# Projecting the keys and values of the last attention during the routing stage before it

## The chip, the cores and the metric

The kernel runs on one core of one Trainium2 chip. The metric is the device time of one execution in microseconds (us); three runs of the kernel before gave 3404.11 to 3409.8, with a median of 3405.26.

## The reference, cut to what matters

A stream `x` of 16 batches, 112 tokens and 256 features passes four layers, each an attention to a fixed context and a feed-forward part. The kernel computes them as eight stages, one after the other. The change is in stage 5 (a feed-forward part with routed experts) and stage 6 (the attention of the fourth layer, here the narrow attention: 16 heads of 16 features, against 64 features in the wide attention of stage 4).

```
x = x + L2_ffn(layernorm(x))                       # stage 5: top 2 of 8 experts for each token
x = x + L3_xattn(layernorm(x), ctx, ctx, mask)     # stage 6

# L3_xattn, per batch; ctx is 375 x 256 and is an input, D_K = 16
q = query @ Wq.T + bq
k = ctx @ Wk.T + bk
v = ctx @ Wv.T + bv
scores = q k^T / sqrt(D_K), -1e9 where mask == 0
out = softmax(scores) v, heads joined, @ Wo.T + bo
```

Keys and values depend on the context and the weights alone, not on `x`.

## The kernel before, in words

The program is written engine by engine: in each stage every engine (TensorE `pe`, VectorE `dve`, ScalarE `act`, GpSimd `pool`, SyncE `sp` for the DMAs) has its own list of instructions, and semaphores order them against each other. `after(eng, sem, n)` waits only where `n` is over zero. Between stages stands a barrier of all engines (`core.clear()`). There is no planner: the order on each engine is the order in the code. `each_batch` runs a body for batches 0 and 1, a hardware loop for 2 to 13 and the body twice more.

**Routing** (`route`, L1705) comes before the experts and has its own barrier behind it. SyncE loads the router's weights and fills the DRAM buffer of the experts' rows with zeros in four DMAs (L1768). For each batch TensorE transposes the normalized tokens (L1938) and computes 8 logits a token (L1931); ScalarE evicts the transposes (L1795), VectorE takes the logits. After the last batch VectorE alone finds the best two experts (L1846 to L1856), TensorE multiplies the choices by a triangular matrix and by ones (L1946, L1947), VectorE turns the sums into positions up to the put list (L1919), and GpSimd scatters the tokens by 32 indirect DMAs (L1779). ScalarE has one exponential between (L1799). Then come the expert matmuls (`run_experts`; its first DMA is L2000) and `combine`.

**Narrow attention** (`softmax_attention` with `wide` false, L781). The opening loads the weights (L924), folds the value bias into the output bias (L1281, L1070), and projects batch 0. Then each batch goes through its 16 heads in pairs. For a pair TensorE multiplies scores into two PSUM banks (L1232). VectorE adds the mask and takes the minimum (L1100), after which TensorE may write the next pair's scores into the same banks. ScalarE takes the exponential (L1038), TensorE transposes the probabilities of the pair before (L1242), VectorE copies the transposes to SBUF (L1111), and after every second pair TensorE multiplies four heads of transposed probabilities by the values (L1258). Those four products write to four different groups of 32 output partitions.

Between these steps stand jobs, at fixed heads in `slots` (L808). They go through two further PSUM banks in turn:

```python
slots = [[K[0]], [], [K[1]], [], [Q[0]], [], [Z], [], [V[0]], [], [Y], [], [V[1]], [], [X], []]
```

K, Q and V project keys, queries and values of the batch after (L1183, L1189, L1194), X transposes the tokens two batches ahead (L1200), Z spreads the reciprocal sums of the batch before and Y multiplies its output by `Wo`. ScalarE evicts K (L999), Q (L1008), V (L1014) and X (L1024), each in its own place between two exponentials. GpSimd spreads the queries into a block-diagonal form (L961), which the scores need. The values lie 32 columns wide for each head, 16 of them zero (memset L953). The last batch has no successor, so no K, Q, V or X job stands in it. SyncE loads context and mask for two batches in turn (L928, L931).

## Time and profile before

| What | Value |
|---|---|
| Median of three runs | 3405.26 us |
| The profiled execution: its time, its span | 3406.88 us, 3404.9 us |
| Mean granted TensorE clock | 0.878 |
| Second routing stage | 2180.0 to 2282.1 |
| Experts and combine of the same layer | 2282.1 to 2702.6 |
| Narrow attention | 2702.6 to 3138.8 |

The stages' borders are where SyncE issues the first DMA of a stage. Times in the rows are us from the span's start. PE is TensorE's matmul, PEld its weight load, DVE VectorE, ACT ScalarE, POOL GpSimd, SPq SyncE's queue. A float32 matmul has two records, so "x8" is four matmuls. In a timeline row stand the start, the time until the last of the merged instructions ends, engine and line, the tiles (out<-in) and, in brackets, the idle time before it with what ended it. [...]

### The profile page before, as it was taken

How to read it: one execution, taken by the hardware profiler on the slowest of the kernel's cores; microseconds unless marked ns; L12 is line 12 of the kernel's file. 1: busy time of each engine (PE TensorE's matmuls, PEld its weight loads, DVE VectorE, ACT ScalarE, POOL GpSimd, SP SyncE). 2: the span in 40 equal slices, each digit the busy share in tenths (PEclk: the TensorE clock that was granted, in tenths of full speed). 3: DMA queues.
4: the chain of work that ended last, by engine and by line, in shares of the span. 5: the costliest groups of instructions: out<-in, count | busy, mean ns of one | idle time of the engine just before them, and what ended most of it. 6: DMA issues, size and time to landing. Idle time of an engine off the chain costs nothing. (4 is left out here: it accounts for less than half of the span.)

```text
span 3404.9 us, 48975 instructions
## 1 busy us (share of the span) xinstructions
PE 2571.2 (76%) x15414; PEld 1780.1 (52%) x15414; DVE 1525.1 (45%) x5311; ACT 1089.5 (32%) x2415; POOL 621.5 (18%) x739
## 2 busy tenths in 40 slices
PE   3775249999478699699999999619996199997232
PEld 3664237777334355356665666418885066665121
DVE  5887612222334443333333333411111666766877
ACT  3443001111079501244444444202221055554121
POOL 0000030000322000144444444330002211111000
PEclk8888569999789889899999999759998599999555
DMA  2111033221121100100000000135553100000000
GB/s 70 45 45 53 29 136 102 78 74 51 50 71 63 51 0 0 65 10 10 5 9 9 9 9 0 66 103 178 184 173 110 53 28 20 24 21 26 0 0 22
DMA packets 62522, 174.60 MB, mean 51 GB/s; under 512 B 13531, under 2 KB 32760, under 8 KB 52952
## 3 DMA queue, kind: packets, MB, share of 16 engines
q1 hardware_dynamic: 52344, 148.58, 13.2%
q0 software_dynamic: 10080, 24.79, 2.3%
q8 instruction: 52, 0.85, 0.1%
q14 instruction: 46, 0.38, 0.0%
HBM read 143.98 MB, written 29.36 MB: 51 GB/s over the span
## 5 line engine op out<-in xcount | busy, mean ns | idle before, releaser
L2131 PE MATMUL L_ffne_up<-L_ffne_xT,L_ffne_wu 128*128 128x280 f32 (+1 forms) x1696 | 406.6, 399 | 23.8 <-DVE L_ffne_xT L2057 15.5
L2131 PEld LDWEIGHTS L_ffne_up<-L_ffne_xT,L_ffne_wu 128*128 128x128 f32 x1696 | 325.6, 193 | 95.2 <-ACT L_ffne_hT L2044 17.5
L1094 DVE TENSOR_REDUCE L_xattn_least<-L_xattn_s 112x1 f32<-112x375 f32 x256 | 128.4, 543 | 440.3 <-PE L_xattn_s L1232 440.3
L948 POOL TENSOR_SCALAR L_xattn_p<-L_xattn_p,L_xattn_rec 112x375 f32<-112x375 f32 x256 | 313.2, 1231 | 0.0
L2117 PE MATMUL L_ffne_dn<-L_ffne_wd,L_ffne_hT 128*128 128x256 f32 (+1 forms) x1312 | 288.1, 379 | 1.6 <-issue 1.6
L1242 PEld LDWEIGHTS L_xattn_pt<-ident,L_xattn_p 112*125 112x125 f32 x1536 | 191.4, 189 | 152.5 <-issue 108.7
L2117 PEld LDWEIGHTS L_ffne_dn<-L_ffne_wd,L_ffne_hT 128*128 128x128 f32 (+1 forms) x1312 | 241.1, 184 | 44.3 <-issue 2.4
L1242 PE MATMUL L_xattn_pt<-ident,L_xattn_p 112*125 112x112 f32 x1536 | 243.3, 291 | 7.6 <-POOL L_xattn_p L948 7.4
L1111 DVE COPY L_xattn_pt<-L_xattn_pt 125x336 f32<-125x336 f32 x512 | 232.7, 495 | 6.4 <-PE L_xattn_pt L1242 6.2
L1183 PE MATMUL L_xattn_job<-L_xattn_ctxT,L_xattn_wk 128*128 128x375 f32 x640 | 221.7, 486 | 1.8 <-ACT L_xattn_xt L1021 0.9
L1194 PE MATMUL L_xattn_job<-L_xattn_wv,L_xattn_ctxT 128*125 128x512 f32 (+1 forms) x576 | 220.1, 523 | 2.1 <-ACT L_xattn_v L1014 0.7
L1038 ACT ACTIVATE L_xattn_p<-L_xattn_s,L_xattn_least 112x375 f32<-112x375 f32 x256 | 145.7, 570 | 188.4 <-DVE L_xattn_least L1094 188.4
L1038 ACT ACTIVATE L_xattn_p<-L_xattn_ssb,L_xattn_least 112x375 f32<-112x375 f32 x256 | 154.4, 603 | 141.3 <-DVE L_xattn_least L1100 134.4
L2020 POOL DMA_DIRECT2D L_ffn_ybuf<-L_ffne_y x82 | 43.8, 535 | 720.0 <-DVE L_ffne_y L2069 405.6
L1100 DVE CUSTOM_DVE_ANT_0 L_xattn_ssb<-L_xattn_s,L_xattn_hide 112x375 f32<-112x375 f32 x256 | 130.8, 544 | 90.4 <-issue 90.4
L2042 ACT ACTIVATE L_ffne_sg<-L_ffne_up 128x280 f32<-128x280 f32 x128 | 51.6, 403 | 349.2 <-PE L_ffne_up L2131 349.2
L2044 ACT ACTIVATE L_ffne_hT<-L_ffne_up,L_ffne_b 128x256 f32<-128x256 f32 x168 | 79.2, 473 | 233.6 <-PE L_ffne_up L2131 231.2
L1258 PE MATMUL L_xattn_o<-L_xattn_pt,L_xattn_v 125*64 125x112 f32 (+1 forms) x3072 | 152.9, 267 | 0.6 <-DVE L_xattn_pt L1111 0.6
L946 POOL TENSOR_TENSOR pool_tick<-ident 1x1 f32<-1x1 f32 x128 | 23.4, 183 | 700.3 <-DVE L_xattn_rec L1106 700.3
L1258 PEld LDWEIGHTS L_xattn_o<-L_xattn_pt,L_xattn_v 125*64 125x64 f32 (+1 forms) x3072 | 110.3, 124 | 76.1 <-issue 56.9
L2087 DVE TENSOR_TENSOR L_ffne_hT<-L_ffne_sg,L_ffne_up 128x280 f32<-128x280 f32 x128 | 57.1, 446 | 205.2 <-ACT L_ffne_sg L2042 205.2
L1183 PEld LDWEIGHTS L_xattn_job<-L_xattn_ctxT,L_xattn_wk 128*128 128x128 f32 x640 | 115.9, 193 | 62.9 <-issue 2.5
(326 smaller groups left out, 4122.7 us busy)
## 6 DMA issues: line engine op xcount, KB each, us to landing
L_ffne_wd<-in_L_ffn_down SPq DMA_DIRECT2D x29, 1024.0 KB, 4.8
L_ffne_wu<-in_L_ffn_up SPq DMA_DIRECT2D x21, 1024.0 KB, 5.5
L_ffne_wu<-in_L_ffn_up SPq DMA_DIRECT2D x8, 2048.0 KB, 7.7
L_xattn_ctxT<-in_ctxT SPq DMA_DIRECT2D x32, 375.0 KB, 3.1
fa_ctxT<-in_ctxT SPq DMA_DIRECT2D x16, 375.0 KB, 6.3
fa_rows<-in_ctx_rows SPq DMA_DIRECT2D x16, 375.0 KB
ta_kT<-in_ctxT SPq DMA_DIRECT2D x16, 375.0 KB
ta_ctxr<-in_ctx_rows SPq DMA_DIRECT2D x16, 375.0 KB
```

Source lines behind the costliest of these rows:

```text
L948: p = pool.tensor_scalar(p_sb[:, head % RP, :], p_sb[:, head % RP, :], rec[:, h, head:head + 1], None, ALU.mult)
L1038: act.activation(p_sb[:, head % RP, :], src, ACT.Exp, bias=least[:, h, head:head + 1], scale=-1.0, accum_out=sums[:, h, head:head + 1]).th ...
L1094: dve.tensor_reduce(low, s, AX.X, ALU.min).then_inc(low_done, 1)
L1100: dve.tensor_tensor_reduce(out=ssb[:, head % 4, :], in0=s, in1=hide[:, h, :], scale=1.0, scalar=3e38, op0=ALU.add, op1=ALU.min, accum_out= ...
L1111: dve.tensor_copy(pt_sb[:, head % RP, :, :], pt_ps[head % 2][0:KP, 0, 0:KT * S].rearrange("p (k s) -> p k s", k=KT)).then_inc(pt_done, 1)
L1183: m = pe.matmul(ps[:, 0, 0:SK], wk[:, c, i * 128:(i + 1) * 128], ctxT[:, h, c, :], start=(c == 0), stop=(c == DC - 1))
L1194: m = pe.matmul(ps[0:KP, 0, n * VW:(n + 1) * VW], ctxT[:, h, c, kt * KP:(kt + 1) * KP], wv[:, c, w * VW:(w + 1) * VW], start=(c == 0), sto ...
L1242: m = pe.transpose(pt_ps[head % 2][0:KP, 0, kt * S:(kt + 1) * S], p_sb[:, head % RP, kt * KP:(kt + 1) * KP], ident[0:S, 0:S])
L1258: m = pe.matmul(o_ps[n * VC:(n + 1) * VC, chunk // 4, chunk % 4 * S:(chunk % 4 + 1) * S], v_sb[:, h, kt, head_at(head + n), :], pt_sb[:, ( ...
L2044: act.activation(hT[:, h, f, q * RH:(q + 1) * RH], src, ACT.Gelu, bias=b1[:, h, f:f + 1]).then_inc(h_done, 1)
L2117: m = pe.matmul(dn_ps[i][0:TR, 0, 0:D], hT[:, h, f, t * TR:(t + 1) * TR], wd[:, h, f, :], start=(f == 0), stop=(f == FC - 1))
L2131: m = pe.matmul(up_ps[s % RING][k][:, 0, 0:RH], wu[:, h, c, k * FF + f * 128:k * FF + (f + 1) * 128], xT[:, h, c, q * RH:(q + 1) * RH], st ...
```

## The change

A class `KeysValues` holds keys and values of all 16 batches in SBUF (97,152 bytes on a partition). The second routing stage opens it: SyncE loads the key and value weights and the context of two batches ahead of the zero fills, and the other 14 behind them. TensorE projects batches 0 and 1 between the last logits and the cumulative matmuls, and the other 14 after these; ScalarE evicts batches 0 and 1 ahead of the exponential of the gaps. In the narrow attention the jobs K and V go, and with them the context loads, the `wk` and `wv` loads and GpSimd's memset of the values. The products read 16 columns of values for each head; VectorE clears the output bank once in their place. TensorE's body is written out for all 16 batches instead of looping, since it addresses keys and values by batch. The job Q waits for the X job's eviction, which the K job did before. The bodies on the other engines keep their loops.

```diff
@@ -805,7 +806,7 @@
         slots = [[K[0]], [K[1]], [K[2]], [K[3]], [K[4]], [K[5], K[6]], [K[7]], [], [Q[0]], [Q[1]], [Y],
                  [V[0]], [V[1], V[2]], [V[3]], [V[4], V[5]], [X]]
     else:
-        slots = [[K[0]], [], [K[1]], [], [Q[0]], [], [Z], [], [V[0]], [], [Y], [], [V[1]], [], [X], []]
+        slots = [[], [], [], [], [Q[0]], [], [Z], [], [], [], [Y], [], [], [], [X], []]
     order = [j for jobs in slots for j in jobs]
     LT = 4 if wide else 2
     LP = 6
...
@@ -912,29 +914,29 @@
         with nc.Block() as block:
             @block.sync
             def _(sp):
-                loads = [(wq[:, :, :], ins[pre + "_Wq"]), (wk[:, :, :], ins[pre + "_Wk"]),
-                         (wv[:, :, :], ins[pre + "_Wv"]), (wo[:, :, :], ins[pre + "_Wo"]),
+                loads = [(wq[:, :, :], ins[pre + "_Wq"]), (wo[:, :, :], ins[pre + "_Wo"]),
                          (bias_y[:, :], ins[pre + "_bo"].partition_broadcast(S))]
                 if wide:
+                    loads += [(wk[:, :, :], ins[pre + "_Wk"]), (wv[:, :, :], ins[pre + "_Wv"])]
                     loads += [(gb[:, 0, :], ins[pre + "_gamma"]), (gb[:, 1, :], ins[pre + "_beta"]),
                               (gate[:, 0:1], ins["L2_xattn_gate"].partition_broadcast(128))]
                 else:
-                    loads += [(bq[:, :], ins[pre + "_bq"]), (bk[:, :], ins[pre + "_bk"]), (bv[:, :], ins[pre + "_bv"])]
+                    loads += [(bq[:, :], ins[pre + "_bq"]), (bv[:, :], ins[pre + "_bv"])]
                 for to, src in loads:
                     sp.dma_start(to, src).then_inc(w_in, 16)
                 def load(b, h):
-                    after(sp, out["v"], (b - 1) * NV)
-                    sp.dma_start(ctxT[:, h, :, :], ins["ctxT"][b]).then_inc(ctx_in[h], 16)
-                    if not wide:
+                    if wide:
+                        after(sp, out["v"], (b - 1) * NV)
+                        sp.dma_start(ctxT[:, h, :, :], ins["ctxT"][b]).then_inc(ctx_in[h], 16)
+                    else:
                         after(sp, mask_done, b - 1)
                         sp.dma_start(msk[:, h, :], ins["mask"][b]).then_inc(ctx_in[h], 16)
                 each_batch(sp, load)
-            CTX = 16 if wide else 32
-            NLOADS = 8
+            NLOADS = 8 if wide else 5
             def wait_ctx(eng, b, h):
-                eng.wait_ge(ctx_in[h], (b - h) * (CTX // 2) + CTX)
+                eng.wait_ge(ctx_in[h], (b - h) * 8 + 16)
             @block.gpsimd
             def _(pool):
...
@@ -1015,7 +1011,10 @@
                                                ps[0:KP, 0, n * VW:(n + 1) * VW].rearrange("p (h d) -> p h d", h=hs),
                                                ACT.Copy)
                     elif kind == "x":
-                        after(act, out["v"], (b - 1) * NV)
+                        if wide:
+                            after(act, out["v"], (b - 1) * NV)
+                        else:
+                            after(act, out["q"], b - 1)
                         for c in range(DC):
                             if wide:
                                 r = act.activation(xt[:, h, c, :], ps[:, 0, c * S:(c + 1) * S], ACT.Identity,
...
@@ -1066,6 +1065,7 @@
                     ch.link(dve.tensor_scalar(bias_y[:, :], bias_y[:, :], gate[0:S, 1:2], None, ALU.mult))
                 else:
                     dve.wait_ge(w_in, NLOADS * 16)
+                    dve.memset(o_ps[:, 0, :], 0.0).then_inc(pad_done, 1)
                     dve.wait_ge(bias_out, 1)
                     dve.tensor_tensor(bias_y[:, :], job_ps[0][0:S, 0, 0:D], bias_y[:, :], ALU.add).then_inc(bias_done, 1)
                     dve.wait_ge(bias_done, 1)
...
@@ -1183,6 +1183,8 @@
                             m = pe.matmul(ps[:, 0, 0:SK], wk[:, c, i * 128:(i + 1) * 128], ctxT[:, h, c, :],
                                           start=(c == 0), stop=(c == DC - 1))
                     elif kind == "q":
+                        if not wide:
+                            pe.wait_ge(done["x"], b + 1)
                         for n in range(QB):
                             for c in range(DC):
                                 at = (i * QB + n) * 128
...
@@ -1228,7 +1230,7 @@
                         if wide:
                             q, k = qt[r, h, n // 2, :], kt_sb[r, h, n // 2, :]
                         else:
-                            q, k = qbd[r, h, n // HG, n % HG // 2, :], kt_sb[r, h, n // HG, :]
+                            q, k = qbd[r, h, n // HG, n % HG // 2, :], keys.kt[r, b, n // HG, :]
                         m = pe.matmul(s_ps[n % 2][0:S, 0, 0:SK], q, k, start=True, stop=True)
                     m.then_inc(s_out, 2)
...
@@ -1255,8 +1257,10 @@
                     chunk = head // SIDE
                     for kt in range(KT):
                         for n in range(SIDE):
-                            m = pe.matmul(o_ps[n * VC:(n + 1) * VC, chunk // 4, chunk % 4 * S:(chunk % 4 + 1) * S],
-                                          v_sb[:, h, kt, head_at(head + n), :], pt_sb[:, (head + n) % RP, kt, :],
+                            hd = head_at(head + n)
+                            v = v_sb[:, h, kt, hd, :] if wide else keys.v[:, b, kt, hd * dh:(hd + 1) * dh]
+                            m = pe.matmul(o_ps[n * VC:n * VC + dh, chunk // 4, chunk % 4 * S:(chunk % 4 + 1) * S],
+                                          v, pt_sb[:, (head + n) % RP, kt, :],
                                           start=(kt == 0), stop=(kt == KT - 1))
                     m.then_inc(pv_out, SIDE)
@@ -1282,9 +1286,14 @@
                                       start=(c == 0), stop=(c == OC - 1))
                     m.then_inc(bias_out, 1)
                     pe.wait_ge(bias_done, 1)
+                    pe.wait_ge(pad_done, 1)
                 pe.wait_ge(xn_done, 1)
                 projections(job)
-                each_batch(pe, body)
+                if wide:
+                    each_batch(pe, body)
+                else:
+                    for b in range(NB):
+                        body(b, b % 2)
                 for head in range(LT):
                     turn_p(NB - 1, 1, H + head - LT)
                 for head in range(10 if wide else 12, H, SIDE):
...
@@ -1675,6 +1684,67 @@
                         m.then_inc(dn_out, 1)
+class KeysValues:
+
+
+    def __init__(self, core, ctx, pre):
+        self.pre = pre
+        self.kt = core.sb(ctx, pre + "_kt", [128, NB, DC, SK])
+        self.v = core.sb(ctx, pre + "_v", [KP, NB, KT, D])
+
+    def open(self, core, ctx):
+
+        pre = self.pre + "kv_"
+        self.wk, self.wv = core.sb(ctx, pre + "wk", [128, DC, D]), core.sb(ctx, pre + "wv", [128, DC, D])
+        self.bk = core.sb(ctx, pre + "bk", [128, DC])
+        self.ctxT = core.sb(ctx, pre + "ctxT", [128, 2, DC, SK])
+        self.ps = [core.banks(ctx, f"{pre}ps{i}", 1) for i in range(2)]
+        self.w_in, self.ctx_in = core.sem(ctx, pre + "w_in"), [core.sem(ctx, f"{pre}ctx_in{i}") for i in range(2)]
+        self.out, self.done = core.sem(ctx, pre + "out"), core.sem(ctx, pre + "done")
+        self.parts = [("k", 0), ("k", 1), ("v", (0, 1)), ("v", (2,))]
+
+    def load_weights(self, sp, ins):
+        for to, src in ((self.wk, "_Wk"), (self.wv, "_Wv")):
+            sp.dma_start(to[:, :, :], ins[self.pre + src]).then_inc(self.w_in, 16)
+        sp.dma_start(self.bk[:, :], ins[self.pre + "_bk"]).then_inc(self.w_in, 16)
+
+    def load(self, sp, ins, b):
+        n = len(self.parts)
+        after(sp, self.out, (b - 1) * n)
+        sp.dma_start(self.ctxT[:, b % 2, :, :], ins["ctxT"][b]).then_inc(self.ctx_in[b % 2], 16)
+
+    def project(self, pe, b):
+
+        h, n = b % 2, len(self.parts)
+        pe.wait_ge(self.ctx_in[h], (b - h) * 8 + 16)
+        for i, (kind, part) in enumerate(self.parts):
+            after(pe, self.done, b * n + i - 1)
+            ps = self.ps[i % 2]
+            if kind == "k":
+                for c in range(DC):
+                    m = pe.matmul(ps[:, 0, 0:SK], self.wk[:, c, part * 128:(part + 1) * 128], self.ctxT[:, h, c, :],
+                                  start=(c == 0), stop=(c == DC - 1))
+            else:
+                for at, kt in enumerate(part):
+                    for c in range(DC):
+                        m = pe.matmul(ps[0:KP, 0, at * D:(at + 1) * D], self.ctxT[:, h, c, kt * KP:(kt + 1) * KP],
+                                      self.wv[:, c, :], start=(c == 0), stop=(c == DC - 1))
+            m.then_inc(self.out, 1)
+
+    def take(self, act, b):
+
+        n = len(self.parts)
+        for i, (kind, part) in enumerate(self.parts):
+            act.wait_ge(self.out, b * n + i + 1)
+            ps = self.ps[i % 2]
+            if kind == "k":
+                r = act.activation(self.kt[:, b, part, :], ps[:, 0, 0:SK], ACT.Identity, bias=self.bk[:, part:part + 1])
+            else:
+                r = act.activation(self.v[:, b, part[0]:part[0] + len(part), :].rearrange("p k d -> p (k d)"),
+                                   ps[0:KP, 0, 0:len(part) * D], ACT.Copy)
+            r.then_inc(self.done, 1)
+
+
 class Routing:
...
@@ -1762,11 +1835,18 @@
                 else:
                     sp.dma_start(more[:, :], ins[pre + "_router_b"].partition_broadcast(S)).then_inc(w_in, 16)
+                if keys:
+                    keys.load_weights(sp, ins)
+                    keys.load(sp, ins, 0)
+                    keys.load(sp, ins, 1)
                 sp.wait_ge(setup, 2)
                 flat = r.xbuf.rearrange("(p n) d -> p (n d)", p=128)
                 for q in range(4):
                     sp.dma_start(flat[:, q * fill_w:(q + 1) * fill_w], zeros[:, :]).then_inc(filled, 16)
                 sp.wait_ge(filled, 64)
+                if keys:
+                    for b in range(2, NB):
+                        keys.load(sp, ins, b)
             @block.gpsimd
             def _(pool):
@@ -1795,8 +1875,15 @@
                     act.activation(xt[:, h, :, :], xt_ps[h][:, 0, 0:DC * S].rearrange("p (c s) -> p c s", c=DC),
                                    ACT.Copy).then_inc(x_done, 1)
                 each_batch(act, body)
+                if keys:
+                    act.wait_ge(keys.w_in, 48)
+                    for b in range(FIRST):
+                        keys.take(act, b)
                 act.wait_ge(gap_done, 1)
                 act.activation(gap[:, :], gap[:, :], ACT.Exp).then_inc(gap_exp, 1)
+                if keys:
+                    for b in range(FIRST, NB):
+                        keys.take(act, b)
             @block.vector
             def _(dve):
@@ -1941,10 +2028,17 @@
                         logits(b - 1, 1 - h)
                 each_batch(pe, body)
                 logits(NB - 1, 1)
+                if keys:
+                    pe.wait_ge(keys.w_in, 48)
+                    for b in range(FIRST):
+                        keys.project(pe, b)
                 pe.wait_ge(picked_done, 1)
                 flat = picked[:, :, :].rearrange("p b e -> p (b e)")
                 pe.matmul(cum_ps[0:S, 0, 0:NE], before[:, :], flat, start=True, stop=True)
                 pe.matmul(cum_ps[0:S, 1, 0:NE], ones[:, :], flat, start=True, stop=True).then_inc(cum_out, 1)
+                if keys:
+                    for b in range(FIRST, NB):
+                        keys.project(pe, b)
 def run_experts(core, pre, r, gated):
...
@@ -2243,6 +2337,14 @@
         for layer in LAYERS:
             PARTS[layer](core)
             core.clear()
+        with ExitStack() as kept:
+            keys = KeysValues(core, kept, "L3_xattn")
+            routed_experts(core, "L2_ffn", False, keys)
+            core.clear()
+            softmax_attention(core, "L3_xattn", keys)
+            core.clear()
+        ternary_ffn(core)
+        core.clear()
         store_output(core, out)
...
```

## Rows read from the trace of the kernel before

**Rows 1.** Windows: us; busy us (xcount) of PE, PEld, DVE, ACT, POOL; PEclk; DMA.
```profile
2219.30:2282.10 62.80, 1.20 (x5) 0.88 (x4) 13.31 (x99) 0.55 (x2) 30.23 (x32) 0.50 0.20 59
2725.06:3108.23 383.17, 381.09 (x3284) 248.20 (x3283) 264.18 (x1084) 206.54 (x630) 63.69 (x59) 1.00 0.07 21
3108.23:3126.46 18.23, 16.62 (x162) 10.79 (x158) 15.19 (x65) 9.12 (x28) 1.04 (x1) 1.00 0.01 1
```

**Rows 2.** Timeline of the second routing stage's end: start, busy time, engine, line.
```profile
2217.74 1.57 PE L1931 MATMUL L_ffnr_lg<-L_ffnr_wr,L_ffnr_xt 128*112 128x8 f32 x8
...
2234.65 0.18 DVE L1919 CAST L_ffn_put<-L_ffnr_slot 112x32 uint32<-112x32 f32 x1
...
2274.47 0.94 POOL L1779 DMA_INDIRECT L_ffn_xbuf<-L_ffn_xf,L_ffn_put  x1 [0.30 <-issue]
2282.10 0.40 SPq L2000 DMA_DIRECT2D L_ffne_rows<-L_ffn_xbuf  x1
```

**Rows 3.** Timeline of TensorE over one looped batch of the narrow attention.
```profile
2850.14 0.89 PE L1232 MATMUL L_xattn_s<-L_xattn_kt,L_xattn_qbd 64*112 64x375 f32 x4
...
2851.70 1.44 PE L1183 MATMUL L_xattn_job<-L_xattn_ctxT,L_xattn_wk 128*128 128x375 f32 x4
2853.07 0.89 PE L1232 MATMUL L_xattn_s<-L_xattn_kt,L_xattn_qbd 64*112 64x375 f32 x4
...
2856.89 0.89 PE L1232 MATMUL L_xattn_s<-L_xattn_kt,L_xattn_qbd 64*112 64x375 f32 x4
...
2862.89 0.89 PE L1232 MATMUL L_xattn_s<-L_xattn_kt,L_xattn_qbd 64*112 64x375 f32 x4
...
2864.45 1.90 PE L1194 MATMUL L_xattn_job<-L_xattn_wv,L_xattn_ctxT 128*125 128x256 f32 x8
2866.28 0.89 PE L1232 MATMUL L_xattn_s<-L_xattn_kt,L_xattn_qbd 64*112 64x375 f32 x4
...
2870.64 0.89 PE L1232 MATMUL L_xattn_s<-L_xattn_kt,L_xattn_qbd 64*112 64x375 f32 x4
...
2872.20 1.04 PE L1194 MATMUL L_xattn_job<-L_xattn_wv,L_xattn_ctxT 128*125 128x256 f32 x4
2873.41 0.89 PE L1232 MATMUL L_xattn_s<-L_xattn_kt,L_xattn_qbd 64*112 64x375 f32 x4 [0.17 <-DVE L_xattn_least L1100]
...
2875.25 0.78 PE L1258 MATMUL L_xattn_o<-L_xattn_pt,L_xattn_v 125*32 125x112 f32 x24
2876.00 0.89 PE L1232 MATMUL L_xattn_s<-L_xattn_kt,L_xattn_qbd 64*112 64x375 f32 x4
```

**Rows 4.** The same view over the stage's last batch.
```profile
3108.23 0.89 PE L1232 MATMUL L_xattn_s<-L_xattn_kt,L_xattn_qbd 64*112 64x375 f32 x4
...
3110.26 0.89 PE L1232 MATMUL L_xattn_s<-L_xattn_kt,L_xattn_qbd 64*112 64x375 f32 x4 [0.30 <-DVE L_xattn_least L1100]
...
3112.62 0.89 PE L1232 MATMUL L_xattn_s<-L_xattn_kt,L_xattn_qbd 64*112 64x375 f32 x4
...
3119.93 0.89 PE L1232 MATMUL L_xattn_s<-L_xattn_kt,L_xattn_qbd 64*112 64x375 f32 x4 [0.30 <-DVE L_xattn_least L1100]
...
3124.03 0.89 PE L1232 MATMUL L_xattn_s<-L_xattn_kt,L_xattn_qbd 64*112 64x375 f32 x4
```

**Rows 5.** Timeline of the narrow attention's opening.
```profile
2710.84 3.75 PE L1281 MATMUL L_xattn_job<-L_xattn_wo,L_xattn_bv 128*112 128x256 f32 x8 [99.58 <-DMA L_xattn_bv<-in_L_xattn_bv]
...
2721.17 1.82 POOL L961 TENSOR_TENSOR L_xattn_qbd<-L_xattn_qt,halfmask 128x448 f32<-128x448 f32 x2 [17.17 <-ACT L_xattn_qt L1008]
```

**Rows 6.** Groups of the narrow attention; DMA issues, the last number is us to landing.
```profile
L999 ACT ACTIVATE L_xattn_kt<-L_xattn_job,L_xattn_bk 128x375 f32<-128x375 f32 x32 | 18.3, 572 | 22.4 <-PE L_xattn_job L1183 22.4
...
L_xattn_ctxT<-in_ctxT SPq DMA_DIRECT2D x32, 375.0 KB, 3.1
fa_ctxT<-in_ctxT SPq DMA_DIRECT2D x16, 375.0 KB, 6.3
...
L_ffn_xbuf<-L_ffnr_zeros SPq DMA_DIRECT2D x4, 1344.0 KB, 10.1
```

More of the change, by code:

```diff
@@ L796, in softmax_attention @@
     VW = 512 if wide else D
-    NK, NQ = IC, IC // QB
-    v_parts = [[(kt, w)] for kt in range(KT) for w in range(inner // VW)] if wide else [[(0, 0), (1, 0)], [(2, 0)]]
+    NK, NQ = IC if wide else 0, IC // QB
+    v_parts = [[(kt, w)] for kt in range(KT) for w in range(inner // VW)] if wide else []
     NV = len(v_parts)
@@ L952, in _ @@
                     return
-                pool.memset(v_sb[:, :, :, :, dh:VC], 0.0).then_inc(setup, 1)
                 def body(b, h):
@@ L994, in job @@
                         after(act, s_out, (b - 1) * H)
-                        to, src = kt_sb[:, h, i, :], ps[:, 0, 0:SK]
-                        if wide:
-                            r = act.activation(to, src, ACT.Copy)
-                        else:
-                            r = act.activation(to, src, ACT.Identity, bias=bk[:, i:i + 1])
+                        r = act.activation(kt_sb[:, h, i, :], ps[:, 0, 0:SK], ACT.Copy)
                     elif kind == "q":
@@ L1248, in products @@
                     pe.wait_ge(pt_done, b * H + head + SIDE)
-                    if head == 0:
+                    if wide and head == 0:
                         pe.wait_ge(done["v"], made("v", b, NV - 1))
```

36 lines of the change are left out of this document (19 added, 17 removed).

## The prediction

> **What bounds the kernel now.** I read the table of windows first, one window for each stage that the change touches. In the narrow attention TensorE is busy 381.09 of 383.17 us at clock 1.00, while VectorE has 264.18 and ScalarE 206.54 [rows 1]. TensorE is the bound there, and the key and value projections are part of what it does. In the second half of the second routing stage it is the other way round: TensorE works 1.20 us in a window of 62.80, at clock 0.50 [rows 1]. What sets the end of that window is a chain: the last logits end at 2217.74 + 1.57 = 2219.3, VectorE writes the put list at 2234.65, GpSimd issues 32 scatters, the last at 2274.47, and SyncE's first DMA of the expert stage goes out at 2282.10 [rows 2]. So the change moves TensorE work from a stage that it bounds into a hole of 62.8 us. The two questions are how much the donor gives back and whether the hole is large enough.
>
> **What one batch of projections costs.** In the looped batch at 2850.14 a key part stretches the distance between two TensorE steps by 2853.07 - 2851.70 = 1.37 us; there are two. The first value part is 2866.28 - 2864.45 = 1.83, the second 1.04 by its row [rows 3]. I take 1.0 for it, since a row's busy time runs a little over the distance. Sum: 2 x 1.37 + 1.83 + 1.0 = 5.57 us a batch at clock 1.00; 16 batches are 89.1 us.
>
> **Narrow attention, what it gives back.** A batch takes 2876.00 - 2850.14 = 25.86 us now [rows 3]. Taking off 5.57 would leave 20.3, but that holds only if TensorE never waits for anything else. The last batch of the stage shows what a batch without these jobs is like, for it has no successor to project for [rows 4]. Its first pair, with no job at all, takes 3110.26 - 3108.23 = 2.03 us, and the next scores stood 0.30 us waiting for VectorE's minimum L1100: scores, two passes of VectorE, scores again are a loop of 2.03 us which no idle TensorE shortens. Pair by pair, before against the last batch:
> - heads 0, 1: 2853.07 - 2850.14 = 2.93 against 2.03; VectorE answers a little later in the loop's body, so I count 2.08: -0.85
> - heads 2, 3: 2856.89 - 2853.07 = 3.82 against 3112.62 - 3110.26 = 2.36: -1.46
> - heads 4 to 7: query and reciprocal jobs stay: 0
> - heads 8, 9: 2866.28 - 2862.89 = 3.39 against 2.03: -1.36
> - heads 10, 11: 2870.64 - 2866.28 = 4.36 against 3124.03 - 3119.93 = 4.10: -0.26, the transposes no longer stall behind a value eviction
> - heads 12, 13: the second value part sits here, but the next scores already waited 0.17 us for VectorE [rows 3], which is at the residual of the batch before. That residual stays: 0
> - heads 14, 15: 0
>
> That is 3.93 us a batch, period 21.9. Fifteen batches carry jobs for a successor: 15 x 3.93 = 59.0. The remaining 1.64 us a batch turn into waits for L1100. The bounds are 3.4 (every light pair held by VectorE for 0.2 us more than in the last batch) and 5.57 (no wait at all): 51 and 84 us.
>
> The prologue: queries of batch 0 stand behind two key parts, and GpSimd's two block-diagonal products, 1.82 us from 2721.17 [rows 5], behind them. Without key parts they start 2.6 us earlier and end at 2720.4; the first scores followed value parts and started at 2725.06, where a window of [rows 1] begins; now they follow GpSimd at once: -4.6. The weight loads shrink by two of 256 KB and the one of the key bias, three issue slots of 0.4 to 0.5 us and a third of the bytes ahead of the bias matmul at 2710.84 [rows 5]: I take -1.9, between 0 and -3. The queries' new wait for their x tile finds it written in the turn before; the memset of the output bank (one VectorE pass, estimated at under 1 us) lies beside the 3.75 us bias matmuls. TensorE now stands some 2.5 us before the first scores and may start them at the lower clock: +1, between 0 and +2. Masks alone are left on SyncE's queue; nobody waited for it. TensorE's body written out sixteen times costs nothing by [rows 3, 4]: the written-out last batch has no gap that another engine doesn't explain.
> Sum of the stage: -59.0 - 4.6 - 1.9 + 1 = -64.5.
>
> **Routing, what it takes.** SyncE issues three weight loads and two context loads ahead of the four zero fills: five slots, 2 to 2.5 us, and 1.3 MB of traffic ahead of them. A fill lands 10.1 us after its issue [rows 6], around 2193, and is needed by the scatters only after 2234.65; 40 us cover it. The context of batches 0 and 1 is in SBUF long before 2219.3. Then the matmuls: 89.1, plus the slow start. The eight 256-column records at 2710.84 took 3.75 us on an engine that came from idling [rows 5]; eight such took 1.90 at clock 1.00 [rows 3]: +1.9. The two cumulative matmuls between batches 1 and 2 are part of 1.20 us at half clock: 0.6. End of the last projection: 2219.3 + 89.1 + 1.9 + 0.6 = 2310.9, its eviction 2311.4, the barrier some 1 us (below 6.7, since 2282.10 - 2275.41 held a landing as well): 2312.4 against 2282.1, +30.3.
> Batches 0 and 1 also stand in front of the cumulative matmuls and, on ScalarE, in front of the exponential of the gaps; VectorE's position chain and then the scatters wait behind these. They take 2 x 5.57 + 1.9 = 13.0 us from 2219.3, so the put list is at most 13 us late and the scatter's end at most at 2295. That is 16 us before TensorE is through: the delay is hidden by the other 14 batches and costs nothing. ScalarE evicts a key part in 0.57 us [rows 6] against the 1.37 that TensorE needs for the next part, so two banks suffice.
> Each context load may start when TensorE takes up the batch before, and has 5.57 us. The attention stages' loads land 3.1 us after issue; those of the first stage, which share the queues with as large a second stream, 6.3 [rows 6]. With a slot of 0.4 that is 3.5 to 6.7 us. The scatters move 112 rows of 1 KB each 1.25 us, 90 GB/s. I take the near row, 3.1: hidden. At the far end it costs (6.7 - 5.57) x 14 = 16 us.
>
> **Sum.** -64.5 + 30.3 = -34.2. The profiled execution took 3406.88 (span 3404.9 and 2 around it): 3372.7. It is 1.6 above the median of 3405.26, so I predict 3371.
>
> **Rivals.**
> *TensorE's time comes back whole.* VectorE's waits shrink with TensorE's, 5.57 a batch: 25 us more, 3346. Against it: the 2.03 us pairs and their wait of 0.30 in the last batch, where nothing else was in the way. Chance 0.05.
> *The context loads bound the projections.* 6.3 us each: 3387. For it: the scatters' descriptors and these loads run at once. Against: 375 KB in 5.57 us are 69 GB/s. Chance 0.10.
> *Slower: the narrow attention falls to half clock.* TensorE, dense now, gets gaps of 0.3 to 1.2 us in three or four pairs of every batch. [...] Against it: the last batch has 16.62 busy of 18.23 us and the granted clock stands at 1.00 [rows 1]. Chance 0.04.
> [...]
> *Slower: the products lose their packing.* The output products now take 16 columns of weights in place of 32. Twelve such matmuls (24 records), at four output offsets, fit into 2876.00 - 2875.25 = 0.75 us today [rows 3]. One by one, at a 256-column record's 1.83 / 8 us scaled to 112 columns, 0.10 each, they would take 2.4: +1.65, four times a batch, 106 over the stage: 3477. It decides against the change from a group time of 0.75 + 34 / 64 = 1.3 us. No row shows 16 columns. Chance 0.03.
>
> **How the numbers follow.** The forecast has 0.75, and by its bounds (attention 51 to 64 us from the pairs, clock and barrier a few us) runs from 3360 to 3382. With the loads' case to the upper side and half of the way to the first rival on the lower one, the range is 3358 to 3388. A kernel that projects as said but gains within 0.2% (7 us, about what a measurement of this kernel can tell from no change), by several small losses: 0.03. Faster 0.75 + 0.05 + 0.10 = 0.90, same 0.03, slower 0.04 + 0.03 = 0.07.
>
> **What would show it.** Expert stage's first DMA at 2312, put list written at 2243 to 2248, TensorE's last projection at about 2311 with clock 1.00 but for its first few us. Period of a narrow batch 21.9, pairs of heads 0, 1 and 8, 9 at 2.03 to 2.2 with waits for L1100. If the period is under 21 the VectorE loop was no bound; if the projections take over 6 us a batch with TensorE waiting for a DMA, the loads are; if the clock of the narrow stage is under 0.95, or a group of twelve products takes over 1 us, one of the slower cases holds.

## The result, and the profile after

The changed kernel takes 3371.47 us, median of four runs (3369.47 to 3374.87), against 3405.22 for the kernel before on the same chip: a ratio of 0.9894, 95% interval 0.9879 to 0.9909, 33.8 us less. Forecast were 3371, range 3358 to 3388, and faster with a chance of 0.90. The profiled execution has a span of 3369.6.

The windows of the changed kernel, one a stage, show where the time went. The columns are those of [rows 1], where PEclk is the TensorE clock that was granted, as a share of its full speed; the first two windows are the second routing stage's first half and its projections, then come the expert combination, the opening of the narrow attention, its batch 0 and its batches 1 to 13 with most of 14 (a batch runs from its first scores to the next batch's).

```profile
2179.16:2218.88 39.72, 19.49 (x96) 17.74 (x97) 13.88 (x48) 7.30 (x18) 2.47 (x2) 0.53 0.45 173
2218.88:2307.99 89.11, 86.45 (x325) 60.38 (x325) 13.43 (x99) 35.41 (x66) 30.24 (x32) 0.98 0.36 102
2644.20:2728.68 84.48, 0.00 (x0) 0.00 (x0) 60.61 (x162) 1.59 (x2) 29.96 (x32) 0.50 0.16 46
2728.68:2743.99 15.31, 5.53 (x21) 3.62 (x21) 1.90 (x5) 3.12 (x9) 1.88 (x3) 0.61 0.28 83
2743.99:2766.06 22.07, 20.32 (x157) 12.64 (x157) 14.16 (x63) 10.57 (x35) 4.72 (x4) 0.75 0.06 16
2766.06:3070.00 303.94, 279.53 (x2796) 185.37 (x2792) 247.62 (x1011) 160.81 (x511) 60.40 (x56) 1.00 0.03 8
```

The hole of [rows 1], 1.20 us of TensorE in 62.80, now holds 86.45 of 89.11 and has grown by what didn't fit. From SyncE's first DMA of a stage to that of the next, before and after:

| stage | before | after | difference | forecast |
|---|---|---|---|---|
| second routing | 102.08 | 128.83 | +26.75 | +30.3 |
| experts and combination | 420.51 | 420.69 | +0.18 | 0 |
| narrow attention | 436.21 | 374.79 | -61.42 | -64.5 |

With 0.9 us less in the stages ahead of the routing and 0.05 more behind the attention the sum is -35.3 (forecast -34.2).

The timeline of the changed kernel's routing stage, against [rows 2] (line numbers have moved: 2018 is the logits, 1725 and 1730 are the key and value projections, 2038 the second cumulative matmul, 2006 the put list, 1859 the scatters, 2094 the first DMA of the experts):

```profile
2217.47 1.56 PE L2018 MATMUL L_ffnr_lg<-L_ffnr_wr,L_ffnr_xt 128*112 128x8 f32 x8
2218.88 4.55 PE L1725 MATMUL L_xattnkv_ps<-L_xattnkv_ctxT,L_xattnkv_wk 128*128 128x375 f32 x8
2223.27 2.75 PE L1730 MATMUL L_xattnkv_ps<-L_xattnkv_wv,L_xattnkv_ctxT 128*125 128x256 f32 x12
2225.94 2.77 PE L1725 MATMUL L_xattnkv_ps<-L_xattnkv_ctxT,L_xattnkv_wk 128*128 128x375 f32 x8
...
2231.35 0.38 PE L2038 MATMUL L_ffnr_cum<-L_ffnr_picked,L_ffnr_ones 112*112 112x128 f32 x2
...
2242.44 0.18 DVE L2006 CAST L_ffn_put<-L_ffnr_slot 112x32 uint32<-112x32 f32 x1
...
2282.28 0.94 POOL L1859 DMA_INDIRECT L_ffn_xbuf<-L_ffn_xf,L_ffn_put  x1 [0.30 <-issue]
...
2299.98 2.77 PE L1725 MATMUL L_xattnkv_ps<-L_xattnkv_ctxT,L_xattnkv_wk 128*128 128x375 f32 x8
2302.58 2.75 PE L1730 MATMUL L_xattnkv_ps<-L_xattnkv_wv,L_xattnkv_ctxT 128*125 128x256 f32 x12
2307.99 0.40 SPq L2094 DMA_DIRECT2D L_ffne_rows<-L_ffn_xbuf  x1
```

No projection row has a wait. A batch is 2.60 us of key and 2.67 of value parts, start to start: 5.27. The put list is 7.8 us later than before. TensorE ends at 2302.58 + 2.75 = 2305.33, and the next stage begins 2.66 later. The page's table of DMA issues gives the context loads that were in dispute (last number: us from issue to landing):

```profile
L_xattnkv_ctxT<-in_ctxT SPq DMA_DIRECT2D x16, 375.0 KB, 3.3
```

TensorE over one batch in the middle of the narrow attention, against [rows 3]:

```profile
2831.54 0.89 PE L1234 MATMUL L_xattn_s<-L_xattn_kt,L_xattn_qbd 64*112 64x375 f32 x4
...
2833.81 0.89 PE L1234 MATMUL L_xattn_s<-L_xattn_kt,L_xattn_qbd 64*112 64x375 f32 x4 [0.55 <-DVE L_xattn_least L1100]
...
2836.17 0.89 PE L1234 MATMUL L_xattn_s<-L_xattn_kt,L_xattn_qbd 64*112 64x375 f32 x4
...
2842.16 0.89 PE L1234 MATMUL L_xattn_s<-L_xattn_kt,L_xattn_qbd 64*112 64x375 f32 x4
...
2844.18 0.89 PE L1234 MATMUL L_xattn_s<-L_xattn_kt,L_xattn_qbd 64*112 64x375 f32 x4 [0.30 <-DVE L_xattn_least L1100]
...
2848.27 0.89 PE L1234 MATMUL L_xattn_s<-L_xattn_kt,L_xattn_qbd 64*112 64x375 f32 x4
...
2851.05 0.89 PE L1234 MATMUL L_xattn_s<-L_xattn_kt,L_xattn_qbd 64*112 64x375 f32 x4 [1.05 <-DVE L_xattn_least L1100]
...
2852.89 0.77 PE L1262 MATMUL L_xattn_o<-L_xattn_pt,L_xattn_v 125*16 125x112 f32 x24
2853.59 0.89 PE L1234 MATMUL L_xattn_s<-L_xattn_kt,L_xattn_qbd 64*112 64x375 f32 x4
```

The batch takes 22.05 us (25.86 before). Three of its scores wait for VectorE's minimum, 0.55, 0.30 and 1.05 us; before, one did, 0.17. A group of products takes 0.77.

The opening, against [rows 5]:

```profile
2734.32 3.73 PE L1285 MATMUL L_xattn_job<-L_xattn_wo,L_xattn_bv 128*112 128x256 f32 x8 [97.32 <-DMA L_xattn_bv<-in_L_xattn_bv]
...
2743.99 1.60 PE L1234 MATMUL L_xattn_s<-L_xattn_kt,L_xattn_qbd 64*112 64x375 f32 x4 [2.40 <-POOL L_xattn_qbd L961]
2746.72 1.59 PE L1234 MATMUL L_xattn_s<-L_xattn_kt,L_xattn_qbd 64*112 64x375 f32 x4 [1.14 <-DVE L_xattn_least L1100]
...
2754.55 1.07 PE L1234 MATMUL L_xattn_s<-L_xattn_kt,L_xattn_qbd 64*112 64x375 f32 x4
```

TensorE waits 2.40 us for GpSimd and then issues scores of 1.60 us in place of 0.89: the lower of the two levels that the profile shows, 0.50 and 1.00, until 2754.97, 11 us later. The wait isn't what brought that level. The windows of the last queries and of the transposes behind them, both ahead of the wait, show it:

```profile
2740.18:2741.31 1.13, 1.13 (x10) 1.12 (x10) 0.00 (x0) 0.00 (x0) 0.00 (x0) 1.00 0.02 7
2741.32:2741.59 0.27, 0.27 (x3) 0.00 (x0) 0.00 (x0) 0.23 (x1) 0.00 (x0) 0.50 0.00 0
```

The granted clock (third figure from the end) falls from 1.00 to 0.50 at 2741.31, while TensorE works.

### The profile page after: what moved, and what is told of

The parts are those of the page before. It is cut to its first block and busy times, and to the rows that moved or that the text cites. A ratio compares the mean times of both kernels' runs of the same rounds, so it can differ in the third digit from the quotient of the medians.

```text
span 3369.6 us, 48589 instructions
## 1 busy us (share of the span) xinstructions
PE 2570.4 (76%) x15414; PEld 1784.2 (53%) x15414; DVE 1526.9 (45%) x5312; ACT 1090.1 (32%) x2399; POOL 620.0 (18%) x738
## 3 DMA queue, kind: packets, MB, share of 16 engines
q8 instruction: 70, 1.15, 0.1%
## 5 line engine op out<-in xcount | busy, mean ns | idle before, releaser
L1183 PE MATMUL L_xattn_job<-L_xattn_ctxT,L_xattn_wk 128*128 128x375 f32 x512 | 175.5, 486 | 1.3 <-ACT L_xattn_xt L1020 0.9
L1196 PE MATMUL L_xattn_job<-L_xattn_wv,L_xattn_ctxT 128*125 128x512 f32 x384 | 172.8, 593 | 0.6 <-ACT L_xattn_qt L999 0.6
L1234 PE MATMUL L_xattn_s<-L_xattn_kt,L_xattn_qbd 64*112 64x375 f32 x512 | 116.0, 530 | 30.8 <-DVE L_xattn_least L1100 28.4
```

The lines of the kernel that those rows point to most:

```text
L1183: m = pe.matmul(ps[:, 0, 0:SK], wk[:, c, i * 128:(i + 1) * 128], ctxT[:, h, c, :], start=(c == 0), stop=(c == DC - 1))
L1196: m = pe.matmul(ps[0:KP, 0, n * VW:(n + 1) * VW], ctxT[:, h, c, kt * KP:(kt + 1) * KP], wv[:, c, w * VW:(w + 1) * VW], start=(c == 0), sto ...
L1234: m = pe.matmul(s_ps[n % 2][0:S, 0, 0:SK], q, k, start=True, stop=True)
```

## The experiments

Each kernel is the changed one with one edit, unless said otherwise. On their chips the kernel before took 3407.3 to 3407.8, so the changed kernel, by its ratio, about 3371.5. Stages are measured as in the table above.

**Where the put list stands.** The number of batches projected ahead of the cumulative matmuls (and ahead of the exponential on ScalarE) is one constant.

```
-        FIRST = 2
+        FIRST = 0        # second kernel: 10
```

> All 16 batches of projections stand behind the cumulative matmuls (none between the last logits and them), the rest as changed. My theory: the routing stage now ends with TensorE, and the scatter is done some 18 us earlier, so an earlier put list buys nothing, while TensorE stands idle from the last logits until the choices are there (5.7 us in the kernel before) and does the cumulative matmuls at half clock: 3371.5 + 6 to 7 = 3378. Rival, the delayed put list (8 us later than before) costs time: 3363.

> Ten batches in place of two stand ahead of the cumulative matmuls. My theory gives the delay of the scatter a cover of 18 us: ten batches move the cumulative matmuls from 2231.1 to 2273.3 (8 x 5.27), the put list to 2284.7, the last scatter to 2325, the next stage to 2332 against 2308: +24, 3395. Rival, the order makes no difference since TensorE's sum of work is the same: 3371.

With 0: 3377.05, ratio 0.9908 (0.9892 to 0.9923), routing stage 135.29, 6.46 more than the changed kernel. With 10: 3395.9, ratio 0.9961 (0.9948 to 0.9975), stage 152.85, 24.0 more. With 0, TensorE stands 5.68 us until VectorE has its picks, so the two batches ahead of the cumulative matmuls fill a wait. With 10 the order of the last events has turned; the timeline of its stage end:

```profile
2325.29 0.94 POOL L1859 DMA_INDIRECT L_ffn_xbuf<-L_ffn_xf,L_ffn_put  x1 [0.30 <-issue]
2332.90 0.40 SPq L2094 DMA_DIRECT2D L_ffne_rows<-L_ffn_xbuf  x1
```

From the last scatter's end to the next stage are 2332.90 - 2326.23 = 6.67 us, as before the change (6.69, [rows 2]). So two chains run beside each other, TensorE's projections with 2.66 us behind them, and put list, scatters and 6.7 behind them; the later one sets the end. In the changed kernel the second would have allowed 2283.22 + 6.7 = 2289.9. The put list has 18 us to spare.

**The hole is too small by four batches.** The last four batches are projected in the combination stage, where TensorE does nothing in 84.48 us.

```
-                    for b in range(FIRST, NB):
+                    for b in range(FIRST, 12):
 ...
+            @block.tensor            # in the combination stage
+            def _(pe):
+                pe.wait_ge(keys.w_in, 48)
+                for b in range(12, NB):
+                    keys.project(pe, b)
```

(The loads and the evictions are divided in the same way, and the combination stage loads both weights again.)

> Batches 0 to 11 are projected in the routing stage, batches 12 to 15 in the combining stage behind the experts, where TensorE does nothing for 84 us. My theory: four batches less take 21.1 us from TensorE, whose end falls behind the scatter's; the scatter's last issue at 2282.28 + 0.94 and the tail of 6.7 us seen before set the next stage at 2290: -18, and the combining stage hides its four batches: 3353. Rival 1, the combining stage pays for them (loads of 375 KB beside the gathers, TensorE at half clock): -18 + up to 20, 3373. Rival 2, the routing stage does not end earlier since the context loads slow the scatter: 3371.

3353.94, ratio 0.9842 (0.9829 to 0.9856). The windows of its four stages, routing, experts, combination, attention:

```profile
2177.97:2288.64 110.67, 84.86 (x340) 63.37 (x340) 27.30 (x147) 34.26 (x68) 32.70 (x34) 0.80 0.40 131
2288.64:2625.06 336.42, 308.42 (x1428) 266.26 (x1428) 33.78 (x84) 80.62 (x169) 22.76 (x42) 0.98 0.51 172
2625.06:2709.58 84.52, 25.16 (x80) 17.12 (x80) 60.14 (x162) 9.89 (x18) 30.09 (x32) 0.64 0.25 71
2709.58:3088.24 378.66, 335.76 (x3240) 221.85 (x3240) 287.80 (x1171) 188.44 (x595) 69.13 (x64) 0.96 0.04 11
```

Routing gives back 18.16 us and the combination, with 25 us of TensorE in it, is 0.04 longer. The attention is 3.9 longer: 0.9 in its opening and 1.5 in batch 0 (23.54 us against 22.07), where the low clock (0.50) holds for 14.2 us from the first scores, until 2740.07, and another 1.5 in its last few us, where the clock fell at 3081.41, 6.8 us ahead of the stage's end (in the changed kernel at 3103.12, 0.4 ahead).

**Keys alone.** The values stay in the attention's batches as before the change.

```
-        slots = [[], [], [], [], [Q[0]], [], [Z], [], [], [], [Y], [], [], [], [X], []]
+        slots = [[], [], [], [], [Q[0]], [], [Z], [], [V[0]], [], [Y], [], [V[1]], [], [X], []]
-        self.parts = [("k", 0), ("k", 1), ("v", (0, 1)), ("v", (2,))]
+        self.parts = [("k", 0), ("k", 1)]
 ...
```

(The context loads, the `wv` load, the memset and the 32-column products come back with the value jobs.)

> Only the keys are projected in the routing stage; the value jobs, their context loads and the 32-column products stay in the narrow attention as before. TensorE's loop is written out as in the changed kernel. My theory: 16 x 2.6 us of key matmuls lie wholly beside the scatter, routing costs about 3 us (two batches ahead of the cumulative matmuls), heads 0, 1 go from 2.93 to 2.28 and heads 2, 3 from 3.82 to 2.35 (15 x 2.1 = 32), the opening gives 3.5: 3372, as much as the whole change. Rival, the gain goes by the TensorE time that leaves the narrow attention: half of 34, 3388.

3376.27, ratio 0.9904 (0.9888 to 0.9919). Routing is 3.46 longer than before the change, as expected. The looped batch takes 23.67, 2.19 less than 25.86, also as expected; but the stage gives 25.8 us and not 35. Batches 1 to 14 give 30.9. The opening, from which the theory had 3.5 us, gives none: the first scores start 23.18 us after the stage's first DMA (22.45 before), batch 0 takes 23.79 in place of 21.91, and from the last batch's first scores to the stage's end are 33.06 (30.59), where the clock falls at 3104.73. The opening:

```profile
2719.76 3.78 PE L1197 MATMUL L_xattn_job<-L_xattn_wv,L_xattn_ctxT 128*125 128x256 f32 x8 [0.69 <-ACT L_xattn_qt L1006]
...
2726.66 1.59 PE L1235 MATMUL L_xattn_s<-L_xattn_kt,L_xattn_qbd 64*112 64x375 f32 x4
```

The value part of batch 0 takes 3.78 where it took 1.99 before the change: TensorE's opening stays at the low clock, 0.50 up to 2736. That the missing key parts are the reason isn't shown. The low level is there ahead of their place (the first transposes take 0.60 us against 0.38), and in the changed kernel, which has no key parts there either, the queries run at 1.00. The profile is also that of the slowest of four executions (3381.61, 5.3 over the median), so the others need not have lost as much at the two ends. The time of 3376.27 lies nearer to the theory's 3372 than to the rival's 3388.

**Does TensorE have slack in the light pairs?** One 256-column matmul (0.53 us from its start to the next) is added to three slots of each batch: first those of heads 0, 8, 12, whose following scores wait for VectorE; then those of heads 2, 6, 10, where none was thought to wait. It writes into the second of the two output banks, which the narrow attention doesn't use.

```
+                        if not wide and pair in (0, 8, 12):      # second kernel: (2, 6, 10)
+                            pe.matmul(o_ps[:, 1, 0:256], wq[:, 0, 0:128], wq[:, 1, 0:256], start=True, stop=True)
```

> One matmul of 128 x 256 (0.46 us at full clock, its result unused) is added to TensorE's list in heads 0, 1 and 8, 9 and 12, 13 of every narrow batch, the pairs without a job. My theory: there TensorE waits 0.3 to 0.7 us for VectorE's minimum and the work falls into that wait: 0 to +3 us, 3371 to 3375. Rival, TensorE is still the bound: 3 x 16 x 0.46 = +22, 3393.

> The same matmul in heads 2, 3 and 6, 7 and 10, 11, where TensorE has products or jobs and no wait was seen: my theory +22 us, 3393. Rival, VectorE's or ScalarE's throughput is the bound of the whole batch and any pair has room: under +5.

The light slots: 3372.13, ratio 0.9894 (0.9879 to 0.9909). The periods of the middle batches are 22.13 and 22.04, 0.07 above those of the changed kernel (22.06 and 21.97), for 1.6 us more of matmuls. TensorE isn't the bound there.

The other slots: 3385.62, ratio 0.9936 (0.9922 to 0.995), attention 16.0 us longer where 22 were expected. The pairs with a matmul grew by 0.43 to 0.45, but the one behind heads 10 and 11 shrank. Scores of heads 12 and 14 in this kernel:

```profile
2852.28 0.89 PE L1234 MATMUL L_xattn_s<-L_xattn_kt,L_xattn_qbd 64*112 64x375 f32 x4
...
2854.63 0.89 PE L1234 MATMUL L_xattn_s<-L_xattn_kt,L_xattn_qbd 64*112 64x375 f32 x4 [0.62 <-DVE L_xattn_least L1100]
```

2.35 us with a wait of 0.62, against 2.78 with 1.05 in the changed kernel: VectorE, at the residual, sets the start of these scores, whatever TensorE did before. Of three slots two pay and one is swallowed: 0.45 + 0.45 + 0.43 - 0.43 = 0.90 us a batch, 12.5 over batches 1 to 14. Another 3.4 of the 16.0 stand behind the last batch's first scores, where the clock fell at 3110.20 and the last `Wo` products took 3.73 us in place of 1.95.

**A third bank for scores.** If the loop scores, two minima, scores is what holds the light pairs, a third bank loosens it.

```
-        s_ps = [core.banks(ctx, f"{n_}s{i}", 1) for i in range(2)]
+        s_ps = [core.banks(ctx, f"{n_}s{i}", 1) for i in range(3)]
-                    after(pe, low_done, b * H + pair)
+                    for n in (pair, pair + 1):
+                        after(pe, low_done, <the last head that used this bank>)
 ...
-                    m.then_inc(s_out, 2)
+                        m.then_inc(s_out, 1)
```

(Head 15 takes the bank of head 13. `s_out` tells VectorE that scores are there, now after each head and not after each pair, so the kernel has a second difference besides the bank, which was not tried alone.)

> The narrow attention's scores go through three PSUM banks instead of two (the second output bank is unused there), each head's scores waiting for the minimum of the head three before. My theory: the loop scores, minimum, scores is what holds the light pairs; with one head of slack heads 8, 9 fall from 2.03 to VectorE's own 1.87, heads 0, 1 from 2.28 and 12, 13 from 2.7 by 0.4 to 0.5: about 1.1 us a batch, 16 us, 3355. Rival, VectorE's throughput is the bound in these pairs: no more than 3 us.

3363.2, ratio 0.9867 (0.9852 to 0.9882); attention 367.70, 7.1 shorter, under half of the 16. The scores of heads 8 to 15 in one batch:

```profile
2798.38 0.89 PE L1239 MATMUL L_xattn_s<-L_xattn_kt,L_xattn_qbd 64*112 64x375 f32 x4
2800.03 0.89 PE L1239 MATMUL L_xattn_s<-L_xattn_kt,L_xattn_qbd 64*112 64x375 f32 x4
2804.22 0.89 PE L1239 MATMUL L_xattn_s<-L_xattn_kt,L_xattn_qbd 64*112 64x375 f32 x4
2805.88 0.88 PE L1239 MATMUL L_xattn_s<-L_xattn_kt,L_xattn_qbd 64*112 64x375 f32 x2
2806.99 0.88 PE L1239 MATMUL L_xattn_s<-L_xattn_kt,L_xattn_qbd 64*112 64x375 f32 x2 [0.23 <-DVE L_xattn_least L1101]
```

(Rows between are other tiles.) Heads 8 and 9 now take 2800.03 - 2798.38 = 1.65 where they took 2.02, less than the 1.87 that was expected as VectorE's own, and heads 12 and 13 1.66 where they took 2.78: the loop was real, though whether the bank or the earlier signal opened it is not shown. But heads 14 and 15, the last two rows, rose from 2.55 to 3.65, with a wait of 0.23 for the bank that head 15 shares with 13; heads 2 and 3 rose from 2.35 to 2.74, heads 10 and 11 from 4.08 to 4.19. The batches stand at 21.54 and 21.45 in turn. What holds them now was not separated. TensorE itself is a candidate again: in the batch from 2787.99 to 2809.53 it is busy 21.20 of 21.54 us with this one wait (20.15 of 22.05 in the changed kernel's batch above, with three), VectorE 17.72 and ScalarE 11.65.

**A warm opening.** Nine filler matmuls stand between the queries' projection and the first scores, in GpSimd's time.

```
+                for _ in range(9):
+                    pe.matmul(o_ps[:, 1, 0:S], wq[:, 0, 0:128], xt[:, 0, 0, :], start=True, stop=True)
```

> Nine query-shaped matmuls (2 us, results unused) fill TensorE's wait for GpSimd ahead of the first scores of the narrow attention. My theory: the first three pairs ran at half clock (scores 1.60 us against 0.89) because TensorE had stood 2.4 us before them; they took 10.6 us against 6.9 in a later batch. With the gap filled: -3.5, 3368. Rival, the clock falls anyway: 3371.

3370.09, ratio 0.9887 (0.9872 to 0.9903), too near to the changed kernel's to be told from it; the profile does tell. Attention 371.38, 3.4 shorter. Scores of batch 0 take 0.89 at once (the first one 15.88 us after the stage's first DMA, 0.6 later), the batch 18.11 against 22.07:

```profile
2743.48 3.80 PE L1294 MATMUL L_xattn_o<-L_xattn_xt,L_xattn_wq 128*128 128x112 f32 x18
2747.21 0.89 PE L1234 MATMUL L_xattn_s<-L_xattn_kt,L_xattn_qbd 64*112 64x375 f32 x4
```

The gain is as the theory has it, the reason it gives is not. The windows of this kernel from its queries to the fillers, and of the fillers:

```profile
2742.31:2743.61 1.30, 1.30 (x12) 1.30 (x13) 0.00 (x0) 0.12 (x1) 0.00 (x0) 1.00 0.10 19
2743.63:2747.02 3.39, 3.39 (x19) 3.39 (x17) 0.00 (x0) 2.04 (x5) 2.78 (x3) 0.50 0.00 0
```

The clock falls here too, at 2743.62, with no wait for GpSimd ahead of it, and the fillers themselves run at the lower level. What they change is when it comes back: at 2747.03, ahead of the first scores, and not in the middle of batch 0.

**The written-out body.** The kernel before with TensorE's body of the narrow attention written out sixteen times, and nothing else.

```
-                each_batch(pe, body)
+                for b in range(NB):
+                    body(b, b % 2)
```

> The kernel before with one edit alone: TensorE's body of the narrow attention is written out sixteen times instead of looped over pairs of batches; projections, projected keys and order stay. Theory (the loop's turn costs nothing): narrow attention 436 us as before, looped batch period 25.83 to 25.88, time within 0.2% of the kernel before, 3402 to 3410, ratio 0.998 to 1.002. Rival (part of the 61.4 us that the changed kernel gained came from writing the body out, the turn of the loop costing 0.3 to 1 us of TensorE's time each second batch): period 25.7 or less on average, 2 to 8 us less, ratio under 0.999. Second rival (straight code is fetched more slowly than a loop): period longer, above 26, ratio over 1.001.

3407.91 (11 runs) against 3407.82, ratio 0.9997 (0.9988 to 1.0006). Two starts of a batch:

```profile
2853.54 0.89 PE L1232 MATMUL L_xattn_s<-L_xattn_kt,L_xattn_qbd 64*112 64x375 f32 x4
...
2879.37 0.89 PE L1232 MATMUL L_xattn_s<-L_xattn_kt,L_xattn_qbd 64*112 64x375 f32 x4
```

The period is 25.83. The loop's turn costs nothing, and all of the attention's gain is the change's. (The stage took 438.1 us in the profile, 1.9 more than before; its first key parts took 4.36 us against 2.79, at a granted clock of 0.52 but for their first 0.9 us.)

**The three that pay, together.** Batches 12 to 15 in the combination, three banks, and the fillers (into the first half of the now single output bank).

> The changed kernel with three edits together: batches 12 to 15 are projected during the expert combination stage in place of the routing stage, three banks for scores with the wait per bank, and nine filler matmuls ahead of the first scores of the narrow attention. Theory (the gains stand in different places and add): -18 from routing, -7 from the attention loop, -3 to -7 from the opening, which without a filler was 4 us colder after projections in the combination; sum -28 to -32 from the changed kernel, 3340 to 3345, ratio to the kernel before 0.981 to 0.982. Rival (the opening stays at half clock, since the filler has 3.8 us only and the three-bank loop gives the opening's scores no faster start): -22 to -25, 3347 to 3350, ratio 0.983.

3339.85 (3336.91 to 3344.03), ratio 0.9801 (0.9788 to 0.9815): 68 us below the kernel before, 32 below the changed one. Its routing and attention windows:

```profile
2177.36:2288.10 110.74, 84.88 (x340) 63.37 (x340) 27.27 (x147) 34.21 (x68) 32.69 (x34) 0.80 0.40 130
2709.53:3071.61 362.08, 344.55 (x3258) 226.19 (x3258) 284.35 (x1171) 188.27 (x595) 69.07 (x64) 0.99 0.04 11
```

Routing -18.1, attention -12.7 against the changed kernel; experts and combination +0.7. Opening and batch 0 are 4.5 us shorter (batch 0 takes 17.8), the rest of the stage 8.2 together. The low clock of the divided projections' opening is gone; but the full level came at 2719.03 here, 2.9 us ahead of the fillers (2.17 us at that level), so this kernel doesn't show how much of that they did.

## Why the prediction was right, step by step

- **The move pays because donor and hole have different bounds: right.** -61.4 against +26.75.
- **Projections, 5.57 us a batch: 0.30 too high.** It was read from distances between steps in the attention's pairs: 2 x 1.37 for the keys and 2.83 for the values. Back to back they are 2.60 and 2.67, 5.27. Why a part costs more between other steps was not looked into. Sixteen times 0.30 are 4.8 us; the stage came out 3.6 shorter than forecast, since the next step but one took 1.2 back.
- **Slow start +1.9: right.** The first batch took 2225.94 - 2218.88 = 7.06, 1.79 over the others, at a mean granted clock of 0.74 against 1.00 behind it.
- **Barrier 1 us: too low.** With the last eviction it is 2.66 where 1.5 was forecast, 1.2 us the other way.
- **The put list is late and costs nothing: right.** 7.8 us of at most 13, first projections 12.3. It was later by less because VectorE's own chain ran until then. The experiments put the point where it starts to cost between two and ten batches.
- **An exponential behind two batches on ScalarE: hidden, but not counted.** The load of the exponential's table, 1.28 us, ran in idle time before the change (from 2218.36, with the exponential at 2223.61); now it stands right ahead of the exponential and so in the put list's chain, where it is hidden too. The evictions aren't the reason: with `FIRST = 0` none stands between, and the load still comes last, 2223.27 to 2224.56, behind a wait of 5.32 us for VectorE. In the changed kernel the eviction ahead ends at 2231.71, the load runs from 2231.73 and the exponential starts at 2233.02: 1.31 us in all.
- **Loads hidden: right.** They land in 3.3 us, near the row of 3.1 that was taken, not the 6.3 of the other stage. That rival (0.10) is out.
- **A batch of the attention, -3.93: right to 0.1.** Pair by pair in the batch shown: heads 0, 1 -0.66 (forecast -0.85; VectorE is later than in the last batch by more than was allowed), 2, 3 -1.46 (-1.46), 4 to 7 -0.01 (0), 8, 9 -1.37 (-1.36), 10, 11 -0.27 (-0.26), 12, 13 +0.01 (0), 14, 15 -0.05 (0). Sum -3.81. Over batches 1 to 14 it is -54.4 / 14 = -3.89. The last batch of [rows 4] was the model of a batch without these jobs, and it was a good one. That the rest turns into VectorE's waits, and not into time, is shown from both sides: 1.6 us of matmuls put back into the light slots cost 0.07 a batch, and with a third bank (and the earlier signal) heads 0 and 1, 8 and 9, 12 and 13 take 1.66 us each, though part of that comes back in the pairs behind them. The rival that TensorE's time comes back whole (0.05) is out: only with three banks does part of it come, 0.5 us a batch.
- **Opening -6.5: right.** From the stage's first DMA to the first scores 22.45 became 15.31, -7.1: up to the bias matmuls 8.23 became 5.64 (-2.6, forecast -1.9), behind them 14.22 became 9.67 (-4.6, as forecast). The memset of the output bank took 0.49 us from 2734.52, beside the bias matmuls; the estimate was under 1.
- **Cold start +1, between 0 and +2: too low, the one step that failed its own bounds.** Batch 0 should have shrunk like the others, from 21.91 to about 18; it took 22.07, and 18.11 with the fillers: 4.0 us. Forecast was that TensorE, having stood 2.5 us, might start the first scores at the lower clock. It did, but two things were otherwise. The low level held for 11 us of batch 0, over scores, transposes and queries alike. And it had come at 2741.31, ahead of that wait, and came with the fillers in the wait's place as well, so the wait is not its reason; which work would have kept the level is open.
- **The slower rivals.** Half clock in the attention (0.04): that gaps of this size bring the low level was the author's supposition, and no run shows it. The granted clock is 1.00 over 303.94 us, 279.53 of them busy, with waits of 0.3 to 1.05 us in every batch. From 2754.97 to 3103.12, with three such waits in most batches, the level stood at 1.00 and never fell. Lost packing (0.03): the group of products takes 0.77 us with 16 columns, 0.78 with 32.

Errors of both signs nearly cancel: projections -4.8 and opening -0.6, barrier +1.2, periods +0.7 and cold start +3.0. The total was hit more closely than its parts.

## What to carry to other kernels

Work of an engine that bounds one stage can go into a stage where it idles, even if the hole is too small: here 86.45 us of TensorE went into a hole of 62.80, what didn't fit made that stage 26.75 longer, and the donor gave back 61.42, all that its next bound left. Look then for the second hole at once; here four batches moved into an idle stage brought 18 us, more than half as much as the whole change. A batch that already lacks the work, the last of a loop, gives the donor's gain pair by pair, far better than the removed busy time does (3.93 forecast from it and 3.89 measured, against 5.57).

## What the runs showed of the chip that was not expected

- TensorE's low level (granted clock 0.50) came in the opening while the engine worked, ahead of its wait of 2.40 us (at 2741.31; the wait begins at 2741.59), and held over 11 us of batch 0, in which TensorE was busy 20.32 of 22.07 us. With nine fillers in the wait's place it came too, but was gone at 2747.03, ahead of the first scores, and batch 0 took 18.11 us.
- Whether the opening itself is fast differs between kernels, behind the same bias matmuls of 3.65 to 3.76 us, and not by the attention's code: the first query part took 1.15 us in the changed kernel, but 2.05 with keys alone, with the divided projections and with `FIRST = 0`, whose attention is the changed kernel's line for line. The first key parts took 2.79 before the change and 4.36 with the written-out body. What decides stays open, and so does whether two executions of one kernel agree in it, since each kernel has one profile. A few us between two kernels can come from this alone.
- The same holds for the stage's end: in five of the experiments' kernels (divided projections, keys alone, both with extra matmuls, three banks) the clock fell 6.6 to 9.2 us ahead of it, in the changed kernel 0.4 us.
- Weights of 16 columns at four output offsets pack like those of 32: 24 records in 0.77 and 0.78 us.
- The end of the routing stage costs 2.66 us behind the last matmul's end, with the eviction of its result in it, and 6.7 us behind a scatter's.
